# Scaling the attention probabilities on ScalarE instead of GpSimd, with the row-sum powers taken one tile at a time

## What is computed

```python
x = _layernorm(x + _L0_gnn_ref(x, adj, ...))   # masked gram matrix, rows normalised
x = _layernorm(x + _L1_gnn_ref(x, adj, ...))   # graph convolution
x = _layernorm(x + _L2_gnn_ref(x, adj, ...))   # 3 steps of a gated recurrent unit (GRU)
x = _layernorm(x + _L3_gnn_ref(x, adj, ...))   # attention:
    scores = jnp.einsum('bqhd,bkhd->bhqk', q, k) / jnp.sqrt(jnp.float32(HD))
    scores = scores + (1.0 - adj)[None, None, :, :] * -1000000000.0
    attn = jax.nn.softmax(scores, axis=-1)
    out = jnp.einsum('bhqk,bkhd->bqhd', attn, v).reshape(b, n, d)
    return out @ Wo + bo
```

## Time and profile before

| | us |
|---|---|
| median of 3 runs | 2326.69 (2326.36 to 2326.75) |
| the profiled execution | 2327.76 |
| its span in the profile | 2326.0 |
| TensorE busy | 2099.9 (90%) |
| VectorE busy | 1548.3 (67%) |
| ScalarE busy | 1267.0 (54%) |
| GpSimd busy | 979.5 (42%) |

### The profile page before, as it was taken

One profiled execution on the slowest core, in us unless ns is written; L12 is line 12 of the kernel. 1 busy time (PEld: TensorE's weight loads), 2 busy tenths in 40 slices (PEclk: granted clock), 3 DMA queues, 4 the chain that ended last, 5 costly groups with the idle time before them and its releaser, 6 DMA issues.

```text
span 2326.0 us, 34745 instructions
## 1 busy us (share of the span) xinstructions
PE 2099.9 (90%) x12342; PEld 1655.9 (71%) x12342; DVE 1548.3 (67%) x3423; ACT 1267.0 (54%) x2516; POOL 979.5 (42%) x1138
## 2 busy tenths in 40 slices
PE   5888999999999999999999999999999999999965
PEld 4666777777777777777777777777777777777743
DVE  5556676676667667666776767677676767767642
ACT  3235646566564656646465564646556464655644
POOL 3013534445353444535444453444435344443533
PEclk8899999999999999999999999999999999999987
DMA  3003021120202112021120301112030111202030
GB/s 122 1 19 70 7 52 46 37 64 19 63 20 55 46 37 64 19 53 30 52 50 28 73 19 41 42 39 62 19 73 28 37 46 37 64 19 67 16 90 10
DMA packets 65617, 101.16 MB, mean 43 GB/s; under 512 B 11425, under 2 KB 31137, under 8 KB 65441
## 3 DMA queue, kind: packets, MB, share of 16 engines
q1 hardware_dynamic: 65440, 98.87, 16.7%
HBM read 23.34 MB, written 8.39 MB: 14 GB/s over the span
## 4 chain that ended last, share of the span: by engine, by line
PE 62%; DVE 21%; ACT 9%; issue 6%; POOL 2%; DMA 1%; SPq 0%; DVEq 0%; POOLq 0%; ACTq 0%
PE ps L843 12%; PE ps L845 12%; PE ps L844 12%; PE ps L865 11%; PE ps L945 6%; PE ps L931 4%; DVE fa L821 4%; DVE fa L819 3%; DVE stats L627 3%; ACT pT L390 2%; DVE xn L653 2%; ACT fa L395 2%; DVE xn L644 2%; PE ps L957 2%; DVE fa L822 2%
## 5 line engine op out<-in xcount | busy, mean ns | idle before, releaser
L672 DVE CUSTOM_DVE_ANT_0 fa<-ps,mask 128x512 f32<-128x512 f32 x512 | 332.1, 685 | 284.8 <-PE ps L931 284.5
L298 POOL TENSOR_TENSOR rsum<-esum,mhalf 128x2 f32<-128x2 f32 x256 | 199.1, 778 | 756.4 <-ACT fa L395 756.4
L304 POOL TENSOR_SCALAR fa<-fa,rsum 128x512 f32<-128x512 f32 x512 | 421.7, 837 | 53.0 <-POOL rsum L298 53.0
L945 PE MATMUL ps<-ident,fa 128*128 128x128 f32 x2048 | 325.3, 282 | 97.7 <-ACT pT L390 85.7
L390 ACT COPY pT<-ps 128x512 f32<-128x512 f32 x512 | 298.8, 584 | 172.6 <-PE ps L945 172.6
L945 PEld LDWEIGHTS ps<-ident,fa 128*128 128x128 f32 x2048 | 243.6, 143 | 205.3 <-ACT pT L390 89.9
L395 ACT ACTIVATE fa<-fa,nmax 128x512 f32<-128x512 f32 x512 | 366.0, 724 | 32.2 <-DVE nmax L672 32.2
L659 DVE TENSOR_TENSOR ra<-ps,ra 128x512 fp32r<-128x512 f32 x224 | 151.1, 686 | 244.2 <-ACT ra L493 140.6
L865 PE MATMUL ps<-adjT,ra 128*128 128x512 f32 x1024 | 259.6, 407 | 27.5 <-DVE ra L745 25.3
L865 PEld LDWEIGHTS ps<-adjT,ra 128*128 128x128 f32 x1024 | 195.8, 194 | 79.0 <-issue 33.5
L931 PE MATMUL ps<-ra 128*128 128x512 f32 x512 | 179.8, 433 | 4.8 <-DMA ra<-ra 4.7
(11 more groups left out here) (183 smaller groups left out, 4653.1 us busy)
## 6 DMA issues: line engine op xcount, KB each, us to landing
ra<-ra SPq DMA_DIRECT2D x512, 128.0 KB, 2.4
fa<-in_x_T SPq DMA_DIRECT2D x17, 512.0 KB, 4.7
fa<-in_x SPq DMA_DIRECT2D x17, 512.0 KB, 3.9
out<-fa SPq DMA_DIRECT2D x16, 512.0 KB, 2.9
fa<-in_L_gnn_w_w SPq DMA_DIRECT2D x3, 512.0 KB, 8.3
adj_n<-in_adj SPq DMA_DIRECT2D x1, 1024.0 KB, 5.6
fa<-in_L_gnn_u_w SPq DMA_DIRECT2D x2, 256.0 KB, 9.3
fa<-in_L_gnn_Wk SPq DMA_DIRECT2D x1, 256.0 KB, 5.8
```

Source lines behind the costliest of these rows:

```text
L298: nc.gpsimd.tensor_tensor(rsum[:, 2 * k:2 * k + 2], esum[:, 2 * k:2 * k + 2], mhalf[:, 4:6], ALU.pow).then_inc(rs_r, 1)
L304: nc.gpsimd.tensor_scalar(SC[:, g], SC[:, g], rsum[:, 2 * k + u:2 * k + u + 1], 1.0, ALU.mult, ALU.mult).then_inc(nrm, 1)
L672: nc.vector.tensor_tensor_reduce(out=SC[:, s % RING], in0=ps[:, 4 + u], in1=mask[:, 2 * (k % 8 // 4) + u], scale=-1.0, scalar=3.0e38, op0= ...
L945: ins = nc.tensor.transpose(dst[:, a, u * P:(u + 1) * P], SC[:, (2 * k + u) % RING, kt * P:(kt + 1) * P], ident[:, :])
```

## The change

GpSimd's `probabilities` becomes `row_sums`: it takes the power of each tile's sum by itself, as soon as that tile's exponential is done, and no longer touches `SC`. The two scalings follow the two exponentials in ScalarE's queue, as copies whose scale is the column of `rsum`; each waits for its power. Who is called where stays the same. `nrm` is now signalled by ScalarE, and `rs_r` counts tiles instead of pieces. Nothing on TensorE, VectorE or SyncE is altered; line numbers behind the edit shift by five or by one.

```diff
-            def probabilities(b, k):
-                gp.wait_ge(ex, b * TILES + (2 * k + 2))
-                nc.gpsimd.tensor_tensor(rsum[:, 2 * k:2 * k + 2], esum[:, 2 * k:2 * k + 2], mhalf[:, 4:6],
-                                        ALU.pow).then_inc(rs_r, 1)
-                gp.wait_ge(rs_r, b * CHUNKS + (k + 1))
-                settle(gp, "pool")
-                for u in range(2):
-                    g = (2 * k + u) % RING
-                    nc.gpsimd.tensor_scalar(SC[:, g], SC[:, g], rsum[:, 2 * k + u:2 * k + u + 1], 1.0,
-                                            ALU.mult, ALU.mult).then_inc(nrm, 1)
+            def row_sums(b, k):
+                for s in (2 * k, 2 * k + 1):
+                    gp.wait_ge(ex, b * TILES + (s + 1))
+                    nc.gpsimd.tensor_tensor(rsum[:, s:s + 1], esum[:, s:s + 1], mhalf[:, 4:5],
+                                            ALU.pow).then_inc(rs_r, 1)
...
                         nc.scalar.activation(SC[:, s % RING], SC[:, s % RING], ACT.Exp, bias=nmax[:, s:s + 1],
                                              scale=-1.0, accum_out=esum[:, s:s + 1]).then_inc(ex, 1)
+                    for s in (2 * k, 2 * k + 1):
+                        act.wait_ge(rs_r, b * TILES + (s + 1))
+                        nc.scalar.activation(SC[:, s % RING], SC[:, s % RING], ACT.Copy,
+                                             scale=rsum[:, s:s + 1]).then_inc(nrm, 1)
```

More of the change, by code:

```diff
@@ L318, in body @@
                 if o is not None:
-                    probabilities(o, 15)
+                    row_sums(o, 15)
                 if t is not None:
@@ L330, in body @@
                 if t is not None:
-                    probabilities(t, 0)
+                    row_sums(t, 0)
                 if i is not None:
@@ L335, in body @@
                     for k in range(1, 6):
-                        probabilities(t, k)
+                        row_sums(t, k)
                 if o is not None:
```

## The result

The changed kernel takes 2474.46 us (median, 2472.62 to 2476.76), the kernel before 2326.72 beside it: a ratio of 1.0635, 95% interval 1.0617 to 1.0654. The forecast was 2438.7 us: the sign is right and the time lies in the range, but of 148 us more, 36 were not foreseen. The profiled execution took 2472.62 us, 1.8 less than the median.

A forecast was written before the change was run, and what follows sets the result against it. TensorE, busy 90%, with roughly 9 us of waits per pass whose chain runs through ScalarE's queue. 2327.8 + 100 (15 passes of 6.7) + 12 (tail) = 2439.8, forecast 2438.7 us for the median; range 2390 to 2485.

The forecast's parts named there:

- The price of a piece: Each piece (two score tiles) holds ScalarE 1.4 us longer: 1.24 of copying, 0.15 of waiting; bounds 1.0 and 1.7.
- Step 0: First GRU step: pieces 4 and 5 stand before the final tanh, less 0.7 from DVE; +2.0 us (1.5 to 2.6).
- The relief of 0.7: DVE operations like L821, no longer stretched beside GpSimd's scalings, give back 0.7 us per GRU step, 2.1 per pass.
- Step 1: Second GRU step: pieces 6 and 7 ahead of casts +0.8, pieces 8 to 10 +0.6; +1.5 us (0.8 to 2.5).
- Step 2: Third GRU step: tanh 2.7 late, DVE gives 0.7 back, piece 15 delays transposes 1.2; +3.2 us (2.2 to 4.0).
- powers are stretched: Rival: powers of pieces 8, 9, 12 and 13 meet DVE's chain and take 0.5 us longer; 2463 us, chance 0.14.
- Tail: Attention running alone at the end: ScalarE's copies queue behind 1.4 us more per piece; +12 us (5 to 22).
- The clock: Rival: longer waits of step 2 bring TensorE's lower clock into passes, about 3 us each; 2485 us, chance 0.03.
- Gaps: Rival: ScalarE's gaps absorb the cost except in step 0 and half of step 2; 2377 us, chance 0.12.
- Faster: Rival: DVE's relief and TensorE's waits for scalings are gained, ScalarE's additions stay off the path; 2283 us, chance 0.04.
- no change: Rival: passes stay set by TensorE's own 128.0 us, its 9 us of waits absorb the shifts; 2327 us, chance 0.03.
- the rule weighed: GpSimd and DVE take a shared port pair as exclusive lock per instruction, the loser fully blocks; L821's 0.37 seemed too small.

The follow-up runs named there:

- the constant scale: Changed kernel with each scaled copy on ScalarE taking a column of ones as scale, waiting for its own exponential and no power: 2410.41 us, ratio 1.0365.
- 4 and 5: Kernel before with pieces 4 and 5 alone scaled by ScalarE right behind their exponentials, one power per tile: 2374.36 us, ratio 1.0203.
- the five in gaps: Kernel before with pieces 0, 1, 2, 3 and 11 scaled by ScalarE right behind their exponentials: 2324.93 us, ratio 0.9995.
- experiments 3 and 5: 3: changed kernel, piece 15's scaled copies behind piece 13's second pT copy, 2440.16 us. 5: that plus `xT_lo` behind piece 14's powers on GpSimd, 2425.39 us.

## Why the prediction was right, and where it fell short

- **The price of a piece: right.** 0.72 us for a copy (722 ns), 1.4 us on ScalarE per piece (1.39 at 1820.56 to 1823.36), a wait of 0.15 for a power. ScalarE is 64% busy and not near 70%: 326 us more, since neighbours overlap and count once, on a longer span. The Trainium skill, "ScalarE: Activation LUTs", section "What ACT_TABLE_LOAD costs", gives 280 ns + 0.833 ns per column with one pointer operand, by which 706 ns would be the estimate here, and an overlap of 93 ns between neighbours; the trace's 722 ns are 16 more.
- **Step 0: right.** +2.0 forecast, +1.9 measured; the tanh 2.66 late (2.7). The relief of 0.7 is confirmed by two kernels (0.77 without scaling, 0.76 with piece 5 moved), though L821 was stretched in only 45 of its 96 cases before.
- **Step 1: right.** +1.5 forecast, +1.4 measured, and by the way forecast: against the step's gather the tanh of r comes 0.9 later (0.8 forecast for the casts ahead of it) and the last tanh 2.2 (2.2). By the constant scale, 0.9 of it are the waits for powers and 0.5 the copies.
- **Step 2: the mechanisms right, the sum short.** "2.7 - 0.7 + 1.2: +3.2" came out as 3.3 + 0 + 1.15 = 4.4. The tanh starts 21.95 us behind the gather, 18.66 before: 0.6 more than the 2.7, as much as the wait at 1877.23 for the stretched power of piece 12 (the rival "powers are stretched", at one piece of the four named there). And "DVE gives 0.7 back" is the step that failed: the relief was credited to a path that in this step runs through the tanh, the `pT` copies and the transposes behind L1167, not through L821. From the tanh to the last transposes are 7.32 us against 6.17, and the wait ahead of them is 1.69, where the forecast's sign was about 3.
- **Tail: +12 forecast, +20 measured**, inside its bounds of 5 and 22, near the end at which every piece pays its 1.4 in full. Pieces don't pay alike there either (5.0 us for 4 and 5, 1.4 for the five in gaps), and no run divides the 20 by cause.
- **The clock: left out of the sum.** It was a rival of 3% with 3 us per pass for every pass. It came as a part of the forecast case, 1 us per pass on average, 15 us more than before has, most of it at the end of step 2; with the wait there taken away (experiments 3 and 5) no pass loses time at that place. As a rival it was wrong in form: a forecast with a new wait in front of TensorE's own work should have carried a term for it.
- **Gaps: half right.** Pieces 0 to 3 and 11 are free, as said. "Faster" and "no change" fell with the first pass. The rival that gaps absorb all but half fell too: they absorb five pieces.

Together: 113 for the passes instead of 100, 20 instead of 12, 15 instead of nothing, less the 3 of the start, and 2 because the profiled execution is shorter than the median.

On the rule weighed: VectorE's L820, which was L821 before, takes 691 to 694 ns in all 96 cases once no scaling runs beside it. The prediction held the 0.37 us against the lock of the Trainium skill's "SBUF — State Buffer", section "SBUF: two separate sides", because they are less than a whole scaling. That was a misreading. The rows of before, GpSimd and VectorE one scaling at a time:

```profile
1186.54 1.11 POOL L304 TENSOR_SCALAR fa<-fa,rsum 128x512 f32<-128x512 f32 x1 [0.21 <-POOL rsum L298]
1187.12 1.06 DVE L821 SCALAR_TENSOR_TENSOR fa<-fa 128x512 f32<-128x512 f32 x1
...
1187.63 1.12 POOL L304 TENSOR_SCALAR fa<-fa,rsum 128x512 f32<-128x512 f32 x1
1188.22 1.06 DVE L822 SCALAR_TENSOR_TENSOR fa<-fa 128x512 f32<-128x512 f32 x1
```

The ends alternate, 1187.65, 1188.18, 1188.75 and 1189.28, each 0.53 to 0.57 behind the other engine's. An instruction that starts while the other engine's is under way loses what is left of that one, and not its whole length; that agrees with one holder at a time. So does a power at 1876.02 that took 0.63 longer, about one VectorE operation of 0.68.

## What to carry to other kernels

Work moved to an engine that is idle on average is priced by the place in its queue: here the same two copies cost 1 us, or nothing, and the idle time ahead of the next instruction that others wait for tells which. A gain elsewhere (here 0.7 us for VectorE) counts only where that engine's result is what releases the next work; compare the end of each candidate with the start of what follows, also where the profile names no wait. And a new wait of about two microseconds in front of TensorE can cost more than itself, since the clock may fall behind it.

## What the runs showed of the hardware

- TensorE's clock fell behind a wait of 1.89 us in one pass and not behind 1.88 at the same place in another; a product of 0.39 us then took 0.63. Moving two copies away from the end of step 2 took all 23 such stretches out of the passes in one kernel; in another, with the same move and one more, 9 were left, at another place.
- Low-clock stretches can fall on the same place of each pass: two variants had one ahead of step 0's gather in 14 of 15 passes, and its 16 matmuls took 5.09 instead of 3.97 us, while kernels with one or two of the same three pieces moved had 5. A saving of 0.7 us per pass was lost that way.
- A VectorE operation of 0.69 us and a GpSimd scaling of 0.70 that work at the same time take 1.06 and 1.11, and end in turns.
- A GpSimd power over one column takes 0.55 us (543 at the least), over two 0.71; beside VectorE's work it took up to 1.18.
